# Packed attention outputs in a two-layer transformer kernel: two heads in one block of 32 rows, value copy on ScalarE

## The reference

```python
# layer 0 attention (weights with biases), q from the normed x, k and v from the context
scores = jnp.einsum('bthd,bshd->bhts', wq, wk) / jnp.sqrt(jnp.float32(DH))
probs = jax.nn.softmax(scores, axis=-1)
attn = jnp.einsum('bhts,bshd->bthd', probs, wv).reshape(b, t, d)
return attn @ wo_w.T + wo_b
...
# layer 1 attention: the same without biases, with a term by head and position, and a mask
bias = -_slopes(NUM_HEADS)[None, :, None, None] * dist[:, None, :, :]
scores = jnp.where(mask[:, None, :, :] == 0, -jnp.inf, scores + bias)
```

## Time and profile before

| | |
|---|---|
| median of 3 runs | 448.05 us (445.83 to 449.14) |
| the profiled execution | 447.33 us, span 445.5 |
| busy: TensorE / VectorE / ScalarE / GpSimd | 341.8 / 312.7 / 268.5 / 139.7 us |
| share of the span | 77% / 70% / 60% / 31% |
| chain that ended last, by engine | PE 54%, DVE 17%, ACT 11%, issue 8%, POOL 7%, DMA 4% |
| attention of layer 0, about | 10 to 146 us |
| attention of layer 1, about | 232 to 388 us |

### The profile page before, as it was taken

The page is one execution under the profiler, slowest core; times in us unless marked ns, Lnnn a source line. Parts: engine busy times, 40 slices in busy tenths (PEclk is TensorE's granted clock), DMA queues, the critical chain, the costliest instruction groups (busy, mean ns, idle before and its releaser), DMA issues.

```text
span 445.5 us, 9526 instructions
## 1 busy us (share of the span) xinstructions
PE 341.8 (77%) x3230; PEld 204.3 (46%) x3230; DVE 312.7 (70%) x856; ACT 268.5 (60%) x473; POOL 139.7 (31%) x241
## 2 busy tenths in 40 slices
PE   1489999999888417999803349999999898796762
PEld 0233454455345416999801113454454343475651
DVE  5677999999966483558322757999999943268864
ACT  2118888889785103655401127988889776357776
POOL 3433133544202007543068534234544211011000
PEclk9999999999999755999965555999999977889996
DMA  5224342333211303453112201112221000000001
GB/s 142 60 76 129 97 114 74 108 107 88 60 54 57 99 1 93 127 159 69 46 29 72 76 15 56 40 50 60 63 60 47 19 4 4 0 1 13 13 24 47
DMA packets 35920, 27.36 MB, mean 61 GB/s; under 512 B 5936, under 2 KB 31920, under 8 KB 35872
## 3 DMA queue, kind: packets, MB, share of 16 engines
q1 hardware_dynamic: 32896, 23.51, 18.2%
q0 software_dynamic: 1248, 2.56, 2.7%
q10 hardware_dynamic: 1728, 0.66, 0.7%
HBM read 14.19 MB, written 4.13 MB: 41 GB/s over the span
## 4 chain that ended last, share of the span: by engine, by line
PE 54%; DVE 17%; ACT 11%; issue 8%; POOL 7%; DMA 4%; SPq 0%; ACTq 0%; DVEq 0%; POOLq 0%
PE M L338 14%; PE S L287 10%; DVE nm L656 8%; PE S L1219 5%; PE S L1238 5%; ACT Pt L513 3%; PE S L1384 3%; POOL Pt L1143 3%; PE M L446 3%; PE M L454 2%; PE M L346 2%; ACT spike L1446 2%; POOL xn L625 1%; PE S L1408 1%; DMA wq<-in_wq 1%
## 5 line engine op out<-in xcount | busy, mean ns | idle before, releaser
L656 DVE TENSOR_REDUCE nm<-S 128x2 f32<-128x512 f32 x256 | 164.7, 686 | 36.2 <-PE S L287 31.8
L513 ACT ACTIVATE Pt<-S 128x1024 f32<-128x1024 f32 x128 | 130.3, 1018 | 35.6 <-PE S L296 33.4
L287 PE MATMUL S<-Kt,Qt 32*128 32x256 f16 x512 | 86.5, 303 | 19.7 <-DMA Qt<-q_lo 9.8
L296 PE MATMUL S<-Qt,Kt 32*128 32x256 f16 x512 | 79.1, 291 | 0.0
L338 PE MATMUL M<-Pt,Vt 128*32 128x256 f32 x1024 | 73.2, 406 | 1.6 <-ACT Osb L500 0.9
L287 PEld LDWEIGHTS S<-Kt,Qt 32*128 32x128 f16 x512 | 25.2, 95 | 75.1 <-DVE nm L656 45.2
L338 PEld LDWEIGHTS M<-Pt,Vt 128*32 128x32 f32 x1024 | 27.7, 113 | 29.0 <-ACT Osb L500 5.5
L632 POOL TENSOR_TENSOR rstd<-ve,mhalf 128x2 f32<-128x2 f32 x26 | 19.3, 742 | 67.8 <-DVE ve L610 67.2
L1264 ACT ACTIVATE hf<-S,b1c 128x128 f32<-128x128 f32 x92 | 26.1, 369 | 17.7 <-PE S L1219 17.5
L801 POOL TENSOR_TENSOR q_lo<-qf,q_hi 128x256 f16<-128x256 f32 x16 | 10.7, 671 | 71.9 <-ACT q_hi L546 71.8
L1136 POOL DMA_INDIRECT xt<-normed_x,source x23 | 22.2, 966 | 34.4 <-DVE source L1054 17.0
(11 more groups left out here) (171 smaller groups left out, 570.2 us busy)
## 6 DMA issues: line engine op xcount, KB each, us to landing
w_ff<-in_w SPq DMA_DIRECT2D x8, 512.0 KB, 3.9
ctxT<-in_ctxT SPq DMA_DIRECT2D x16, 128.0 KB, 2.6
Pt<-in_mask SPq DMA_DIRECT2D x8, 256.0 KB
Qt<-q_hi SPq DMA_DIRECT2D x28, 64.0 KB, 1.9
Kt<-k_hi SPq DMA_DIRECT2D x28, 64.0 KB, 1.9
sorted_y<-ysb SPq DMA_DIRECT2D x23, 64.0 KB
Kt<-k_lo SPq DMA_DIRECT2D x16, 64.0 KB, 1.9
Qt<-q_const SPq DMA_DIRECT2D x16, 64.0 KB, 3.4
```

Of the source, the lines that this page charges most:

```text
L287: mm = pe.matmul(S1[h % 2][:, q, :], Qt[b % NBUF][rows_of(h), h // HG, q * P:(q + 1) * P], Kt[b % NBUF][rows_of(h), h // HG, :], start=Tru ...
L296: mm = pe.matmul(S2[pair % 2][:, hh, k, :], Kt[b % NBUF][rows_of(h), h // HG, k * P:(k + 1) * P], Qt[b % NBUF][rows_of(h), h // HG, :], st ...
L513: act.activation(Pt[i // 2][:, 2 * j:2 * j + 2, :].rearrange("p a n -> p (a n)"), S2[i % 2][:, :, :, :].rearrange("p a k n -> p (a k n)"), ...
L656: v.tensor_reduce(nm[par][:, h // 8, :, h % HG, h // HG % 2], S1[h % 2][:, :, :], AX.X, ALU.max, negate=True)\
```

## The change

Two heads now share a block of 32 rows. The value tile gets a gap: each group of four heads is followed by 16 zero columns, and for the odd groups the 32 columns that `pv` takes begin 16 before the head's values. So the head of an even group writes rows 0 to 15 of a block and zeros in 16 to 31, the head of an odd group adds zeros and its own rows 16 to 31. Groups 0 and 1 accumulate in columns 0 to 255 of bank M1, groups 2 and 3 in columns 256 to 511. `pv` has as many products as before.

```diff
-        Vt = [sb(f"Vt{i}", [P, QT, H, 32]) for i in range(2)]
+        Vt = [sb(f"Vt{i}", [P, QT * NPK, 2, HG * KB + KH]) for i in range(2)]
+        Vflat = [v[:, :, :, :].rearrange("p a g r -> p (a g r)") for v in Vt]
+        Vheads = [v[:, :, :, 0:HG * KB].rearrange("p a g (i r) -> p (a g) i r", r=KB) for v in Vt]
...
             def pv(b, par, g):
...
-                if g == 0:
-                    pe.wait_ge(ly["v_copied"], b + 1)
+                tile, sub = g // 2, g % 2
                 for k in range(QT):
                     for i in range(HG):
-                        mm = pe.matmul(M[O_BANK[g]][32 * i:32 * i + 32, 0:S], Vt[par][:, k, HG * g + i, :],
-                                       Pt[g][:, i, k * S:(k + 1) * S], start=(k == 0), stop=(k == QT - 1))
+                        at = (k * NPK + tile) * 2 * (HG * KB + KH) + sub * HG * KB + i * KB
+                        mm = pe.matmul(M[1][KB * i:KB * i + KB, tile * S:(tile + 1) * S], Vflat[par][:, at:at + KB],
+                                       Pt[g][:, i, k * S:(k + 1) * S], start=(sub == 0 and k == 0),
+                                       stop=(sub == 1 and k == QT - 1))
```

```diff
-            def o_copy(b, par, g):
-                act.wait_ge(ly["pv_done"], 4 * b + g + 1)
-                act.activation(Osb[par][:, g, :], M[O_BANK[g]][:, 0:S], ACT.Identity,
+            def o_copy(b, par):
+                act.wait_ge(ly["pv_done"], NG * (b + 1))
+                act.activation(Osb[par][:, :, :].rearrange("p t n -> p (t n)"), M[1][:, :], ACT.Identity,
...
+                    for n in range(QT * NPK):
+                        q, tile = n // NPK, n % NPK
+                        mm = pe.transpose(M[1][:, n * P:(n + 1) * P], Osb[par1][:, tile, q * P:(q + 1) * P], eye[:, :])
+                    mm.then_inc(ly["ot_done"], 1)
```

The copy of the values goes from VectorE (ahead of the maxima of pair 6) to ScalarE (behind exp 6):

```diff
-                    v.tensor_copy(Vt[1 - par][:, :, :, 0:DH], M[0][:, 0:S].rearrange("p (k h d) -> p k h d", k=QT, h=H)) \
-                     .then_inc(ly["v_copied"], 1)
...
+                    act.activation(Vheads[1 - par][:, :, :, 0:DH],
+                                   M[0][:, 0:S].rearrange("p (a i d) -> p a i d", i=HG, d=DH), ACT.Copy) \
+                       .then_inc(ly["v_copied"], 1)
```

More of the change, by code:

```diff
@@ L404, in slot_fn @@
                 if gate:
-                    gate_products(pe, 0, 2)
-                pair(2)
+                    gate_products(pe, 2, 4)
+                pair(3)
+                if old:
+                    pe.wait_ge(ly["ot_norm"], b)
+                    for q in range(QT):
+                        mm = pe.transpose(M[1][:, q * P:(q + 1) * P], attn[:, q, :], eye[:, :])
+                    mm.then_inc(ly["aT_done"], 1)
                 if new:
@@ L421, in slot_fn @@
                               stop=True).then_inc(ly["k_done"], 1)
-                if old:
-                    pe.wait_ge(ly["ot_norm"], 2 * b)
-                    for q in range(QT):
-                        mm = pe.transpose(M[1][:, q * P:(q + 1) * P], attn[:, q, :], eye[:, :])
-                    mm.then_inc(ly["aT_done"], 1)
-                if gate:
-                    gate_products(pe, 4, GATE_AHEAD)
-                pair(4)
-                if ffn and s == B - 1:
-                    ffn_start(ffn, -3)
-                if nxt and ly["bias"]:
+                pair(5)
+                if nxt:
                     next_m_turn()
@@ L439, in slot_fn @@
                     pv(b, par, 0)
-                if nxt and ly["position"]:
-                    next_m_turn()
-                pair(5)
+                pair(6)
                 if nxt:
@@ L530, in slot_fn @@
                 exp(1)
+                exp(2)
                 if new:
@@ L535, in slot_fn @@
                     act.activation(xnT[:, :], M[0][:, 0:S], ACT.Copy).then_inc(ly["xnT_copied"], 1)
-                exp(2)
+                exp(3)
+                gate = s == B and ly["bias"]
+                if gate:
+                    gate_copies(act, 0, 4)
+                if old:
+                    act.wait_ge(ly["aT_done"], b)
+                    if older:
+                        act.wait_ge(ly["op_done"], b - 1)
+                    act.activation(aT[:, :], M[1][:, 0:S], ACT.Copy).then_inc(ly["aT_copied"], 1)
+                if gate:
+                    gate_copies(act, 4, GATE_AHEAD)
                 if new:
@@ L726, in slot_fn @@
                 r(4)
-                if ahead and cur:
-                    norm_moments(v, b + 3, ly["norm_own"], ly["xvar"], applied(b + 3))
+                if old:
+                    v.wait_ge(ly["op_done"], b)
+                    if ly["bias"]:
+                        v.wait_ge(ly["x_biased"], b)
+                    x = X[:, (b - 1) * QT:b * QT, :].rearrange("p q d -> p (q d)")
+                    v.tensor_tensor(x, M[1][:, 0:S], x, ALU.add).then_inc(ly["x_added"], 1)
                 if gathering:
```

151 lines of the change are left out of this document (56 added, 95 removed).

## The result

The changed kernel took 450.18 us (median of 7 runs, 449.76 to 452.78), the kernel before, run beside it, 447.83 (445.83 to 449.60). The ratio on record, formed from fast runs alone and not the quotient of the two medians (1.005), is 1.0102, with a 95% interval of 1.0067 to 1.0137: about 1% slower, where I had forecast 1.1 us less. All 7 times of the changed kernel lie above all 7 of the kernel before. The profiled executions have spans of 448.1 and 445.5 us; I explain their 2.6 us.

A forecast was written before the change was run, and what follows sets the result against it. The prediction took conversion chains and TensorE's queue, not VectorE at 97%, to bound the steps. Its terms, +4.5 + 0.5 - 1.3 - 0.8 - 4 = -1.1, gave 447.0 us against the median, range 438 to 456.

The forecast's parts named there:

- The DMA queue: SyncE's issues, last the rows of turned maxima: later, but still landing in time; costed at nothing, 0.5 a step without cover.
- rows land late: Rival, slower: issues of 1.7 us in most steps make the maxima's rows late, 0.6 for ten steps, 453; chance 0.08.
- Step 0: First step of layer 1, at the lower clock and with no earlier batch: the later conversions cost about 0.
- Layer 1's steady steps: Steps 1 to 5: later conversions delay the turn to 9.96, with 4.5 behind it; 0.9 longer each, +4.5.
- Layer 0's steady steps: Five steps: the turn waits for the key conversion, steps of 13.4 to 13.5 against 13.40; +0.5, within -1.5 and +2.
- The start of layer 1: Pair 5 moves ahead of the turn that waits for `parts`, so its two maxima run during the wait; -1.3.
- The end of layer 0: Three ScalarE copies and one round of turning and normalising leave the path, partly behind the exps; -0.8 (0 to -1.5).
- The end of layer 1: Two rounds of turning and normalising go and the ffn's first work moves back; -4, bounds 6.5 less and -1.
- Prices: Instruction costs: new ScalarE copy 0.60 and 0.68, value copy 0.38; VectorE loses 0.84 of busy time a step.
- VectorE as the bound: Rival, faster: steps shrink by VectorE's 0.7, giving 435, or 441 in part; chance 0.30, including layer 1's end yielding 6.5.
- The clock falls: Rival, slower: the clock drops in steady steps, 2.7 a fall; from three falls on +8, 455; chance 0.20.
- a row of clock near 0.5 inside steps 1 to 5: Sign that the forecast is wrong: granted clock near 0.5 in layer 1's steady steps; no size of its own.

The follow-up runs named there:

- values_before_turn: The changed kernel with pv 0 put back ahead of the turn of the next maxima in layer 1's TensorE order: 449.05 us, ratio 1.0091.
- parts_first: The changed kernel with GpSimd's splitting of the next maxima put ahead of q_lo in layer 1: 451.15 us, ratio 1.0089.
- queries_early: The changed kernel with the projections one pair of scores earlier and ScalarE's copies for them one exponential earlier, as before: 443.02 us, ratio 0.9916.
- values_on_scalar_alone: The kernel before with only the value copy moved from VectorE to ScalarE, ahead of exponential 6: 447.60 us, ratio 1.0006.

## Why the prediction was wrong, point by point

The sum was -1.1 against a measured +2.6 between the profiled executions. Two terms that the prediction put at nothing, the DMA queue and step 0, are more than the whole difference.

**The DMA queue (0).** This is the first step that failed. "I cost it at nothing" rested on a slack of about 0.4 in layer 0, on a landing of 1.8 us, the median of the earlier trace rows, and on issues of 0.6. The slack was nothing: it counted all of the time between landing and use as free, and 0.2 of it passes between a landing and pair 0 in each of the chains read here. Both times have a tail in the kernel before, landings up to 3.7, which the prediction left out, and issues up to 1.7, which it met once and took for chance. Three of ten steady steps met it: 0.88 by a landing of 3.07, 0.90 by an issue of 1.66 and the one behind it, and 0.35 by a landing of 3.06, together +2.1. The rival "rows land late" had the place right, and with its issues of 1.7 the reason of one step in three; it expected them in most steps, and did not have the late landings. In values_before_turn and parts_first the same queue, with the clock, takes the gain away once the wait for GpSimd is lifted: the early conversions had covered two limits at once.

**Step 0 ("about 0").** This is the second. It cost +1.65 in layer 1 and +1.06 in layer 0. I argued with the lower clock and no earlier batch, but pv 0 queued behind the turn is no less late there. values_before_turn, which puts pv 0 alone back, gave 1.35 of layer 1's back, and the two other kernels with layer 1's changed order had 17.07 and 17.18, so that layer 1's loss is well founded. Layer 0's is not: kernels with its order differ by 1.1 there, and their mean, 15.9, is less than 0.5 above the kernel before.

**Layer 1's steady steps (+4.5).** The mechanism was right, in its order and in its places: the turn was put at 9.96 and came at 9.89 (298.69 to 308.58), q_hi's end was put at 7.7 and came at 7.5, and the wait of over 1 us is there. Behind the turn I took 4.5 and it was 4.66 (to 313.24): the value projection took 0.65 and not 0.5, and 0.1 of waiting stood ahead of the next pair 0, while a pair took 0.33, less than the 0.4 assumed. So an undisturbed step is 14.55 to 14.59 and not 14.4: +1.1 and not +0.9. Two of five were not undisturbed: one by a fall of the clock (+0.6 on top), one by a late transfer (the +0.35 above). Together +6.4. queries_early and parts_first show the cause.

**Layer 0's steady steps (+0.5).** Undisturbed ones took 13.51, +0.12 each or +0.6 over five, and TensorE's turn waits 0.51 for kf there, as laid out. With the late transfer and the slow issue it became +2.4.

**The start of layer 1 (-1.3)** measured -1.39, though VectorE's wait there did not go, as foretold, but fell from 5.03 to 3.85. **The end of layer 0 (-0.8)**: -0.6 with the experts behind it, which is not to be told from chance, since that stretch took 129.9 to 132.5 in the ten kernels with the packing. **The end of layer 1 (-4)**: -5.3, inside its bounds, mostly by the order. The ffn behind it, for which the prediction has no term, took 1.4 less; in its first stretch the clock had been low before and was not now.

**Prices.** ScalarE's new copy 0.596 and 0.686 (taken as 0.60 and 0.68), the value copy 0.379 (0.38), the multiply 0.425 for two of 0.292, a saving of 0.16 (0.17). The reciprocal was missed: 0.349 for two of 0.250 saves 0.15, not 0.25. VectorE's saving is 0.73 and not 0.84, which changed nothing.

**VectorE as the bound (0.30).** Refuted by values_on_scalar_alone and queries_early. Part of that chance I gave to layer 1's end yielding its 6.5 in full; it yielded 5.3, and could not outweigh the steps.

**The clock falls (0.20).** It fell in one of ten steady steps, at +0.6, not 2.7, and in the last steps of layer 0, where it had not before (+0.63). The prediction had named a row of clock near 0.5 inside steps 1 to 5 as a sign that it is wrong, and there is one. The rival was real and much smaller than I had priced it.

Had I charged step 0 with its 2.7 and the queue with 2.1, the sum would have been +3.7 and the median forecast 451.8, near the 450.18. That takes the two terms from the result; nothing ahead of it gave their size, only that neither was nothing. The packing itself is worth little in queries_early, at most 0.1 us in a steady step together with the value copy, since copy, transposes and normalising were covered, and 0.9 by one trace at layer 1's end.

## What to carry to other kernels

A change that frees one engine and delays a conversion is judged by the chain behind the conversion, and in each queue it feeds. Ask for the spread of a transfer's landing times and of its issues, not only the median, and compare the longest with the slack left, after taking off what passes between a landing and the work that waits for it. A step that runs at the lower clock pays for a dense stretch that comes late too, and where little is left for TensorE to do, products that nobody reads can cost less than the fall.

## What the runs showed of the hardware

Transfers of 32 KB (the rows) land 1.8 us after their issue at the median and those of 64 KB 1.9. Now and then they took 2.5 to 3.8, from SyncE's queue and from ScalarE's alike (3.78 and 3.81), and SyncE's issues, 0.6 at the median, took 1.0 to 1.9. Almost all of these late ones run beside a 16 KB packet of the queue named "instruction". In layer 0 all ten kernels with the packing had a late landing in the second steady step, and eight of them a slow issue in the third.

TensorE's granted clock fell to 0.50 in stretches with score pairs, transposes and short waits between them, without a long idle one: from 120 to 122 in queries_early, where a fall begins, the profile has it busy for 1.39 of 2 us. Three products more in each of the last two steps removed the fall in all of step 6, in both layers, and made the kernel 3 us faster.
